# State-space layer's weights and tables loaded while the first attention layer runs, and the product of its output weights formed in that layer's drain

## The chip, the cores and the metric

The kernel runs on one NeuronCore of a Trainium2 chip, as one launch. The metric is the device time of that launch in microseconds (us), as the median of three runs. A core has five engines that run side by side and meet only at semaphores: PE (TensorE, matmuls and transposes), DVE (VectorE), ACT (ScalarE), POOL (GpSimd) and SP (SyncE, which here only issues DMA transfers; its issues stand as SPq in the trace). All transfers of this part go through the one queue that SP feeds, and share 16 DMA engines.

## The reference, cut to what matters

The program is four layers over `x` of 32 batches of 512 rows of 256 values. Each takes its input normalised and adds its result to `x`; only the first two touch the change.

```python
# layer 0, attention: one 512x512 table of edge types (adj) for each batch
x = x + _L0_gnn_ref(_layernorm(x, axis=-1), adj, L0_gnn_W, ...)
# layer 0, state space (mamba2)
x = x + _L0_ffn_ref(_layernorm(x, axis=-1), L0_ffn_W_in, L0_ffn_conv_w, L0_ffn_conv_b, L0_ffn_dt_bias,
                    L0_ffn_A_log, L0_ffn_D, L0_ffn_norm_w, L0_ffn_W_out, L0_ffn_W_lin, L0_ffn_b_lin)
...
# the end of the state-space layer: two products with constant matrices, one behind the other
Y = Y * jax.lax.rsqrt(jnp.mean(Y * Y, axis=-1, keepdims=True) + EPS) * norm_w
out = Y @ W_out
return out @ W_lin + b_lin
```

Because `norm_w`, `W_out` and `W_lin` are constant, the kernel forms `Wc = diag(norm_w) W_out W_lin` (512 x 256) once and multiplies by it alone.

## The kernel before

`build` calls five phases in turn: `first_attention_phase` (tiles `g0_...`, shown as `g_...` in the trace), `typed_attention_phase` (`ty_...`, whose body runs only on unusual edge types, and not for these inputs), `state_space_phase` (`ssm_...`), a second attention phase (also `g_...`) and an LSTM phase. Each phase is a block of its own: all engines meet at its end, then POOL clears its semaphores one by one (`Memory.clear`), and only then does the next block begin. Tiles of a phase are given up at its end, so a later phase can't be filled while an earlier one runs, unless its tiles are allocated outside both. Only `kept` lives across the first two.

In every phase each engine runs its own list, `period(b)`, in which operations of several batches are written out in a fixed order by hand; `b.wait(...)` puts a semaphore wait ahead of an operation. No planner sets anything; the order in the code is the order on the engine.

**First attention phase, the parts around the change.** SP, per period k: the edge table of batch k+4 (`load_adj`, L334, 1 MB, into the single buffer `ADJ`, so it waits until DVE and ACT have read the table before it), x of batch k+5 (`load_x`, L329), the result of batch k (`store`, L338). DVE reads `ADJ` in `make_mask` (L647, four 128x512 pieces). At the end, the last batch drains: PE ends with `outputs_turned` (L444), DVE with `squares_sum` (L711), POOL goes on with the layer norm (L806 to L820) and the last store follows. SP then waits for the stores to land, and the block ends.

**State-space phase, its setup.** SP issues x of batch 0 (L1216), then 35 small and large loads through `put` (L1214): all weights, biases and tables, two of them the same 8 values into eight row groups (`dtb`, `rate`), and then x of batch 1 (L1245). Every load of `put` counts on one semaphore, `w`. PE waits for all 35 before its first instruction, transposes `W_out` (L1266), waits for DVE's copies (L1606), and forms `W_out W_lin` (L1271). DVE casts the tables `head_rows` and `below` to bf16 (L1610 to L1614), repeats `Wdt` (L1617), scales the product into `Wc` (L1622), and only behind all this in its own list does it come to the first batch: `norm_stats` (L1632). From there the first batch goes DVE (statistics), POOL (L1816), ACT (normalised x, L1458), PE (L1280). `norm_stats` has its own semaphore for x, `x_loaded`; what keeps it from starting is its place in DVE's list:

```python
v.wait_ge(s["setup_a"], 1)
v.wait_ge(s["setup_v"], 5)
```

## Time and profile before

| | us |
|---|---|
| runs | 4551.28, 4548.48, 4547.19; median 4548.48 |
| profiled execution, its own time | 4549.33 |
| its span | 4547.5 |
| first attention phase, to the issue of its last store | 0 to 1018.3 |
| state-space phase, from its first instruction | 1033.95 |
| second attention phase, from its first instruction | 2417.53 |

The span is what the profiler saw of the engines, and the difference to the execution's own time (1.8 us) lies around it. Over the whole span PE is busy 88%, DVE 76%, ACT 63% and POOL 26% of the time. These shares say nothing on the stretch that the change touches, which is under 1% of the span; there one reads what each engine waited for.

### The profile page before, as it was taken

The numbers are of one execution on the slowest core, as the hardware profiler recorded it, in microseconds if no ns is written. First come the engines' busy times: TensorE is split into PE (matmuls) and PEld (weight loads), VectorE is DVE, ScalarE is ACT, GpSimd is POOL, SyncE is SP. The second block draws the span as 40 slices with busy tenths as digits, with TensorE's granted clock in tenths as the row PEclk, the third lists the DMA queues.
The fourth block names the chain that finished last, engine by engine and source line by source line (L and its number), as shares of the span: only waits on it lengthen the run. The fifth ranks groups of instructions, "written<-read, shape, count | busy, mean of one in ns | idle before, by whom it ended". The sixth has DMA issues, their size and how long they took to land. (4 is left out here: it accounts for less than half of the span.)

```text
span 4547.5 us, 142915 instructions
## 1 busy us (share of the span) xinstructions
PE 3986.8 (88%) x55570; PEld 2859.9 (63%) x55713; DVE 3476.3 (76%) x9096; ACT 2879.7 (63%) x7042; POOL 1181.9 (26%) x1028
## 2 busy tenths in 40 slices
PE   7999999975999999999997999938888888888882
PEld 5666666642666666666666777727777776777772
DVE  6999999975889888988886888825666666666666
ACT  6999999965888888888884777613333332333330
POOL 4777777760222222222221111000000000000000
PEclk9999999987999999999998999969999999999996
DMA  2222222211000000000003333321121111111115
GB/s 65 70 75 65 67 75 75 75 42 52 29 20 29 29 29 20 29 29 29 23 17 97 133 136 136 106 47 40 34 43 34 43 36 42 36 41 37 40 37 162
DMA packets 326430, 252.61 MB, mean 56 GB/s; under 512 B 171388, under 2 KB 289916, under 8 KB 323708
## 3 DMA queue, kind: packets, MB, share of 16 engines
q1 hardware_dynamic: 324220, 235.03, 17.7%
q8 instruction: 448, 7.34, 0.7%
q10 hardware_dynamic: 1536, 8.39, 0.5%
q14 instruction: 226, 1.85, 0.1%
HBM read 159.43 MB, written 67.11 MB: 50 GB/s over the span
## 5 line engine op out<-in xcount | busy, mean ns | idle before, releaser
L2510 PE MATMUL lstm_G_psum<-lstm_Whh,lstm_HT 128*32 128x192 f32 x8192 | 440.0, 332 | 266.8 <-DVE lstm_HT L2687 266.5
L2580 ACT ACTIVATE lstm_TC<-lstm_G_psum 128x192 f32<-128x192 f32 x512 | 170.5, 333 | 706.7 <-PE lstm_G_psum L2510 706.7
L1534 ACT ACTIVATE ssm_EX<-ssm_Z_psum,ssm_tok 128x256 f32<-128x256 f32 (+1 forms) x1024 | 371.8, 423 | 156.1 <-PE ssm_Z_psum L1364 86.3
L2510 PEld LDWEIGHTS lstm_G_psum<-lstm_Whh,lstm_HT 128*32 128x32 f32 x8192 | 214.2, 109 | 353.8 <-DVE lstm_HT L2687 320.2
L2502 PE MATMUL lstm_G_psum<-lstm_Wih,lstm_XT 128*32 128x192 f32 x8192 | 427.9, 327 | 0.0
L2676 DVE SCALAR_TENSOR_TENSOR lstm_AB<-lstm_TC 128x128 f32<-128x128 f32 x512 | 150.2, 293 | 335.1 <-ACT lstm_TC L2580 331.0
L2840 POOL TENSOR_SCALAR lstm_rstd<-lstm_mv 128x4 f32<-128x4 f32 x32 | 7.2, 225 | 1435.2 <-DVE lstm_mv L2670 1435.2
L541 ACT ACTIVATE g_PR<-g_S,g_nmax 128x512 f32<-128x512 f32 x512 | 367.9, 722 | 1.5 <-DVE g_nmax L676 1.5
L683 DVE COPY g_PT<-g_PT_psum 128x512 f32<-128x512 f32 x512 | 344.3, 683 | 26.1 <-PE g_PT_psum L424 21.4
L532 ACT ACTIVATE g_relu<-g_Z_psum,g_src 128x512 f32<-128x512 f32 x512 | 346.0, 682 | 20.5 <-PE g_Z_psum L417 20.4
L676 DVE CUSTOM_DVE_ANT_0 g_S<-g_Z_psum,g_relu 128x512 f32<-128x512 f32 x512 | 345.5, 684 | 10.2 <-ACT g_relu L532 8.6
L424 PEld LDWEIGHTS g_PT_psum<-g_ident,g_PR 128*128 128x128 f32 x2048 | 242.5, 141 | 135.9 <-ACT g_PR L541 53.8
L424 PE MATMUL g_PT_psum<-g_ident,g_PR 128*128 128x128 f32 x2048 | 303.1, 276 | 3.4 <-DVE g_PT L683 3.2
L1290 PE MATMUL ssm_J_psum<-ssm_XT,ssm_W_in 128*128 128x512 f32 x640 | 305.4, 600 | 0.5 <-DVE ssm_CV L1693 0.5
L2588 ACT ACTIVATE lstm_tc<-lstm_TC 128x64 f32<-128x64 f32 x512 | 131.3, 257 | 262.3 <-DVE lstm_TC L2679 262.3
L2502 PEld LDWEIGHTS lstm_G_psum<-lstm_Wih,lstm_XT 128*32 128x32 f32 x8192 | 285.3, 140 | 5.3
L1828 POOL TENSOR_TENSOR ssm_SS<-ssm_SS,ssm_SQ 128x512 f32<-128x512 f32 x96 | 123.8, 1290 | 611.6 <-ACT ssm_SQ L1547 606.6
L2683 DVE SCALAR_TENSOR_TENSOR lstm_H<-lstm_TO,lstm_tc 128x64 f32<-128x64 f32 x512 | 116.4, 227 | 201.6 <-ACT lstm_tc L2588 201.6
L435 PE MATMUL g_O_psum<-g_PT,g_HB 128*64 128x512 f32 x1024 | 262.7, 613 | 0.8 <-DVE g_PT L683 0.8
L1290 PE MATMUL ssm_A_psum<-ssm_XT,ssm_W_in 128*128 128x512 f32 x512 | 244.1, 599 | 1.4 <-DVE ssm_CV L1693 1.4
L1722 DVE SCALAR_TENSOR_TENSOR ssm_M<-ssm_EX,ssm_G 128x768 f32<-128x768 f32 x256 | 242.5, 948 | 0.1
L2058 PE MATMUL g_A_psum<-g_HS,g_PT 128*128 128x256 f32 x1024 | 241.8, 379 | 0.0
(303 smaller groups left out, 10832.6 us busy)
## 6 DMA issues: line engine op xcount, KB each, us to landing
g_ADJ<-in_adj SPq DMA_DIRECT2D x64, 1024.0 KB, 6.5
x<-g_XO SPq DMA_DIRECT2D x64, 512.0 KB, 5.4
g_X<-in_x SPq DMA_DIRECT2D x32, 512.0 KB, 4.3
ssm_X<-x SPq DMA_DIRECT2D x32, 512.0 KB, 3.9
x<-ssm_OUT SPq DMA_DIRECT2D x32, 512.0 KB, 2.9
g_X<-x SPq DMA_DIRECT2D x32, 512.0 KB, 4.4
lstm_raw<-x SPq DMA_DIRECT2D x1024, 16.0 KB, 1.8
lstm_U<-x SPq DMA_DIRECT2D x128, 128.0 KB, 3.5
```

Source lines behind the costliest of these rows:

```text
L424: ins = pe.transpose(PTb[n % 2][:, k * P:(k + 1) * P], PR[n % 4][:, k * P:(k + 1) * P], ident[:, :])
L435: ins = pe.matmul(Ob[hh * E:(hh + 1) * E, :], HB[b.slot][:, k, h * E:(h + 1) * E], PT[h][:, k, :], start=(k == 0), stop=(k == IT - 1), ski ...
L532: act.activation(relu[n % 4][:, :], score_bank(b, n)[:, :], ACT.Relu, scale=(1.0 - ALPHA) / ALPHA, bias=src[b.slot][:, t, HH * p + hh:HH * ...
L541: act.activation(PR[n % 4][:, :], S[n % 4][:, :], ACT.Exp, scale=-1.0, bias=nmax[:, n % 4:n % 4 + 1], accum_out=rsum[b.slot][:, t, HH * p ...
L676: v.tensor_tensor_reduce(S[n % 4][:, :], score_bank(b, n)[:, :], relu[n % 4][:, :], -1.0, 3e38, ALU.add, ALU.min, nmax[:, n % 4:n % 4 + 1] ...
L683: v.tensor_copy(PT[HH * p + hh][:, :, t * P:(t + 1) * P], PTb[n % 2][:, :].rearrange("p (k i) -> p k i", k=IT)).then_inc(s["ev"], 1)
L1290: ins = pe.matmul(BANK[f"p{k}"][:, :], W_in[:, kc, c:c + P], XT[:, kc, :], start=(kc == 0), stop=(kc == KC - 1))
L1534: ins = act.activation(EX[h % NE][:, col:col + n], Zb[c][:, i * CHUNK:i * CHUNK + n], ACT.Exp, bias=tok[b.slot][:, i, c, h:h + 1])
L1722: v.scalar_tensor_tensor(out=M[h % NM][:, :], in0=EX[h % NE][:, :], scalar=1.0, in1=G[b.slot][:, :], op0=ALU.min, op1=ALU.mult).then_inc(s ...
L2058: ins = pe.matmul(BANK[held][:, (t % 2) * D:(t % 2 + 1) * D], PT[t][:, k * P:(k + 1) * P], HS[b.slot][:, k, :], start=(k == 0), stop=(k == ...
L2502: pe.matmul(bank[32 * j:32 * (j + 1), 0:n], XT[c.slot][:, kc, :, t], Wih[:, kc, j, first:last], start=False, stop=False, skip_group_check= ...
L2510: ins = pe.matmul(bank[32 * j:32 * (j + 1), 0:last - first], HT[t % 2][:, 32 * kc:32 * (kc + 1)], Whh[:, kc, j, first:last], start=False, ...
```

## The change

Twelve tiles of the state-space phase (`ident`, `W_in`, `Wdt_rep`, `Wc`, `cw`, `cb`, `skip`, `dtb`, `rate`, `blin`, `keep`, `allowed`) move into a dictionary `ready` that is allocated beside `kept` and lives from the first phase to the end of the state-space phase. SP fills them in the first attention phase: `next_weights` adds 31 loads behind the stores of periods 2 to 12. `W_out` is loaded over `WT`, a tile of the first phase's own setup, and `W_lin` and `norm_w` into new tiles there. Behind its last period PE transposes `W_out` and forms the product, DVE copies and scales it into `Wc`. The tables `head_rows` and `below` are now handed over as bf16 in pairs, so that they are loaded straight into `head_bf` and `rows` by three loads in the state-space phase (655 KB in place of 1.3 MB, no casts); PE waits for these three only in `spread`, its first use. `Wdt` repeated is loaded four times in place of one load and two copies. The state-space phase's DVE begins `norm_stats` behind four memsets and a wait on ACT's exponent of `rate`.

```diff
+        W_lin = m.sb("W_lin", [P, KC, D])
+        WoT = m.sb("WoT", [P, KC, 2 * D])
+        normw = m.sb("normw", [P, 4])
...
+        WT = m.sb("WT", [P, H, D])
+        W_out = WT
...
+            def next_weights(part):
+
+                w_in = nw["W_in"].rearrange("(c k) e -> k c e", k=P)
+                if part == 0:
+                    sp.wait_ge(s["setup_pe"], 2)
+                    put(W_out[:, :, :], nw["W_out"].rearrange("(c k) e -> k c e", k=P))
+                    put(W_lin[:, :, :], nw["W_lin"].rearrange("(c k) e -> k c e", k=P))
+                    put(normw[:, :], nw["norm_w"].rearrange("(c k) -> k c", k=P), allow_slow_non_contiguous=True)
+                if part == 1:
+                    put(nk["W_in"][:, :, :], w_in[:, :, 0:nk["W_in"].shape[2]])
+                if part == 2:
+                    put(nk["allowed"][:, :], consts["allowed"])
+                    put(nk["keep"][:, :], consts["part_masks"])
+                    put(nk["cw"][:, :, :], nw["conv_w"].rearrange("(c k) e -> k c e", k=P))
+                if part == 3:
+                    put(nk["cb"][:, :], nw["conv_b"].rearrange("(c k) -> k c", k=P), allow_slow_non_contiguous=True)
+                    put(nk["blin"][:, :], nw["b_lin"].rearrange("(o d) -> o d", o=1).to_broadcast([P, D]))
+                if part == 4:
+                    for h in range(2):
+                        put(nk["skip"][64 * h:64 * (h + 1), :],
+                            nw["D"].rearrange("(o c h) -> o c h", o=1, h=2)[:, :, h].to_broadcast([64, 4]),
+                            allow_slow_non_contiguous=True)
+                if part in (5, 6):
+                    for r in (0, 1):
+                        k = 2 * (part - 5) + r
+                        put(nk["Wdt_rep"][:, :, 8 * k:8 * (k + 1)], w_in[:, :, nk["W_in"].shape[2]:])
+                if part in (7, 8, 9, 10):
+                    for k in (2 * (part - 7), 2 * (part - 7) + 1):
+                        put(nk["dtb"][8 * k:8 * (k + 1), :], nw["dt_bias"].rearrange("(h o) -> h o", o=1))
+                        put(nk["rate"][8 * k:8 * (k + 1), :], nw["A_log"].rearrange("(h o) -> h o", o=1))
+
             for k in range(-5, nb + 0):
                 period(Batch(None, k, SLOTS))
+                if 2 <= k < 13:
+                    next_weights(k - 2)
+            assert n == N_W
+            sp.wait_ge(s["nw"], 16 * N_W)
...
+            pe.wait_ge(s["nw"], 16 * N_W)
+            pe.wait_ge(s["s"], ITEMS * nb)
+            for kc in range(KC):
+                for c in range(4):
+                    ins = pe.transpose(Zb[kc][:, c * P:(c + 1) * P], W_out[:, c, kc * P:(kc + 1) * P], ident[:, :])
+            ins.then_inc(s["wo_pe"], 1)
+            pe.wait_ge(s["wo"], 2)
+            pe.wait_ge(s["ev"], ITEMS * nb)
+            for c in range(4):
+                for kc in range(KC):
+                    ins = pe.matmul(PTb[c // 2][:, (c % 2) * D:(c % 2 + 1) * D], WoT[:, kc, c * P:(c + 1) * P],
+                                    W_lin[:, kc, :], start=(kc == 0), stop=(kc == KC - 1))
+            ins.then_inc(s["wc_pe"], 1)
...
+            v.wait_ge(s["wo_pe"], 1)
+            for kc in range(KC):
+                v.tensor_copy(WoT[:, kc, :], Zb[kc][:, :]).then_inc(s["wo"], 1)
+            v.wait_ge(s["wc_pe"], 1)
+            for c in range(4):
+                v.tensor_scalar(nk["Wc"][:, c, :], PTb[c // 2][:, (c % 2) * D:(c % 2 + 1) * D], normw[:, c:c + 1], None,
+                                ALU.mult).then_inc(s["wc"], 1)
...
             sp.dma_start(X[0][:, :, :], xv[0]).then_inc(x_loaded[0], 16)
-            put(ident[:, :], consts["identity"])
+            sp.dma_start(head_bf[:, :].bitcast(F32), consts["head_rows"]).then_inc(s["w"], 16)
             for k in range(2):
-                put(allowed[:, 2 * k * P:(2 * k + 1) * P], consts["upto"])
...
+                sp.dma_start(rows[k][ROWS:P, :, :].rearrange("p k l -> p (k l)").bitcast(F32), consts["below"][ROWS:P, :]
+                             ).then_inc(s["w"], 16)
...
             def spread(b, h, c):
+                if b.off == 0 and h == 0:
+                    pe.wait_ge(s["w"], 48)
```

**DVE, from the end of the first attention phase's list into the typed phase, before** (names as in the code, buffer numbers left out):

```order
L711 TENSOR_REDUCE g_ssq<-g_SQ 128x16
L224 UNCONDITIONAL_BRANCH
L968 UNCONDITIONAL_BRANCH
L971 MEMSET ty_ones 128x128
L972 MEMSET ty_half 128x16
```

and now:

```order
L780 TENSOR_REDUCE g_ssq<-g_SQ 128x16
L835 COPY g_WoT<-g_Z_psum 128x512 x2
L838 TENSOR_SCALAR kept_Wc<-g_PT_psum,g_normw 128x256 x4
L232 UNCONDITIONAL_BRANCH
L1045 UNCONDITIONAL_BRANCH
L1048 MEMSET ty_ones 128x128
```

The two copies and the four products with `norm_w` stand behind the last operation of the drain, `squares_sum`.

**DVE, from the start of the state-space phase to its first batch, before:**

```order
L1600 MEMSET ssm_ST 128x512 x2
L1601 MEMSET ssm_ones 128x256
L1602 MEMSET ssm_allowed 128x128
L1603 MEMSET ssm_half 128x16
L1606 COPY ssm_Y<-ssm_Z_psum 128x512 x2
L1610 CAST ssm_head_bf<-ssm_M 128x768 x3
L1610 CAST ssm_head_bf<-ssm_M 128x256
L1612 CAST ssm_rows<-ssm_EX 64x128
...
L1617 COPY ssm_Wdt_rep<-ssm_Wdt 128x32 x2
L1622 TENSOR_SCALAR ssm_Wc<-ssm_J_psum,ssm_normw 128x256 x4
L1632 BN_STATS ssm_stats<-ssm_X 128x6 x4
```

and now:

```order
L1625 MEMSET ssm_ST 128x512 x2
L1626 MEMSET ssm_ones 128x256
L1627 MEMSET ssm_half 128x16
L1634 BN_STATS ssm_stats<-ssm_X 128x6 x4
L1638 BN_AGGR ssm_mv<-ssm_stats 128x2 x4
```

Everything between the memsets and the statistics of batch 0 has left the list.

**SP, around the second period that carries extra loads.** Before, the store of one batch is followed at once by the edge table:

```order
L334 DMA g_ADJ<-in_adj 128x4x512
L329 DMA g_X<-in_x 128x4x256
L338 DMA x<-g_XO 128x4x256
L334 DMA g_ADJ<-in_adj 128x4x512
```

and now, periods 2 and 3:

```order
L358 DMA x<-g_XO 128x4x256
L329 DMA g_WT<-in_L_ffn_W_out 128x4x256
L329 DMA g_W_lin<-in_L_ffn_W_lin 128x2x256
L329 DMA g_normw<-in_L_ffn_norm_w 128x4x1
L354 DMA g_ADJ<-in_adj 128x4x512
L349 DMA g_X<-in_x 128x4x256
L358 DMA x<-g_XO 128x4x256
L329 DMA kept_W_in<-in_L_ffn_W_in 128x2x1152
L354 DMA g_ADJ<-in_adj 128x4x512
```

Between a store and the edge table stand now one to four loads, in eleven periods running.

## Rows read from the trace of the kernel before

**Rows 1.** The page: busy tenths of PE in 40 slices of the span.

```profile
PE   7999999975999999999997999938888888888882
```

**Rows 2.** Waits from 1018 to 1110 us: engine, line, releaser: total, times, longest.

```profile
ACT ssm_rate L1452 <- DMA ssm_rate<-in_L_ffn_A_log: 52.0, 1, 52.0
```

**Rows 3.** Timeline, start of the state-space phase: start, duration, engine and operation.

```profile
1034.09 0.39 SPq L1216 DMA_DIRECT2D ssm_X<-x  x1
...
1035.34 0.07 DVE L1603 MEMSET ssm_half<- 128x16 f32 x1
...
1041.41 3.16 SPq L1214 DMA_DIRECT2D ssm_cb<-in_L_ffn_conv_b  x1
1044.62 2.23 SPq L1214 DMA_DIRECT2D ssm_normw<-in_L_ffn_norm_w  x1
1046.89 1.36 SPq L1214 DMA_DIRECT2D ssm_blin<-in_L_ffn_b_lin  x1
...
1055.49 0.29 SPq L1214 DMA_DIRECT2D ssm_rate<-in_L_ffn_A_log  x1
```

**Rows 4.** Timeline, setup work of the state-space phase and its first batch.

```profile
1058.97 1.97 PE L1266 MATMUL ssm_Z_psum<-ssm_ident,ssm_OUT 128*128 128x128 f32 x8 [32.27 <-DMA ssm_rate<-in_L_ffn_A_log]
1060.97 1.29 DVE L1606 COPY ssm_Y<-ssm_Z_psum 128x512 f32<-128x512 f32 x2 [25.56 <-PE ssm_Z_psum L1266]
...
1062.32 5.16 PE L1271 MATMUL ssm_J_psum<-ssm_Y 128*128 128x256 f32 x16 [1.38 <-DVE ssm_Y L1606]
...
1067.52 1.66 DVE L1622 TENSOR_SCALAR ssm_Wc<-ssm_J_psum,ssm_normw 128x256 f32<-128x256 f32 x4 [2.67 <-PE ssm_J_psum L1271]
1069.27 1.41 DVE L1632 BATCH_NORM_STATS2 ssm_stats<-ssm_X 128x6 f32<-128x256 f32 x4
...
1075.47 1.09 PE L1280 MATMUL ssm_J_psum<-ssm_ident,ssm_XN 128*128 128x128 f32 x4 [7.99 <-ACT ssm_XN L1458]
...
1080.55 1.39 DVE L1632 BATCH_NORM_STATS2 ssm_stats<-ssm_X 128x6 f32<-128x256 f32 x4
...
1102.17 0.33 PE L1359 MATMUL ssm_Z_psum<-ssm_rows,ssm_head_bf 128*128 128x384 bf16 x1
```

**Rows 5.** Tile view of ssm_X, whole span: time from issue to landing.

```profile
DMA to landing us min/median/max: 3.6/3.9/4.0
```

**Rows 6.** Tile view of g_ADJ, 100 to 1000 us, the same.

```profile
DMA to landing us min/median/max: 5.2/5.8/6.6
```

**Rows 7.** Timeline, SP's issues around period 3 of the first phase.

```profile
241.76 0.50 SPq L338 DMA_DIRECT2D x<-g_XO  x1
245.05 0.37 SPq L334 DMA_DIRECT2D g_ADJ<-in_adj  x1
```

**Rows 8.** Timeline, DVE's first read of that edge table.

```profile
254.13 0.52 DVE L647 TENSOR_SCALAR g_MASK<-g_ADJ 128x512 bf16<-128x512 int32 x1
```

**Rows 9.** Stretches: length, busy us of each engine, PEclk, DMA share, GB/s.

```profile
155.00:160.00 5.00, 4.95 (x28) 2.49 (x26) 4.32 (x16) 4.15 (x10) 4.84 (x4) 1.00 1.01 341
...
1045.00:1050.00 5.00, 0.00 (x0) 0.00 (x0) 0.00 (x0) 0.00 (x0) 0.00 (x0) 0.50 0.79 201
```

**Rows 10.** Timeline, drain of the first attention phase.

```profile
998.87 1.42 PE L444 MATMUL g_A_psum<-g_ident,g_OT 128*128 128x128 f32 x8
...
1006.98 1.22 DVE L711 TENSOR_REDUCE g_ssq<-g_SQ 128x16 f32<-128x1024 f32 x1 [3.45 <-ACT g_SQ L560]
...
1015.98 2.34 POOL L820 TENSOR_TENSOR g_XO<-g_G,g_XB 128x1024 f32<-128x1024 f32 x1
1025.49 0.17 DVE L971 MEMSET ty_ones<- 128x128 f32 x1 [17.29 <-PEq L118]
```

**Rows 11.** DMA view, 1018 to 1024 us: KB, us from issue to landing.

```profile
x<-g_XO SPq DMA_DIRECT2D x1, 512.0 KB, 2.9
```

**Rows 12.** Stretches, the state-space phase's first matmuls: columns as in rows 9.

```profile
1072.00:1082.00 10.00, 5.75 (x19) 3.14 (x20) 1.81 (x6) 4.10 (x8) 1.05 (x3) 0.50 0.00 0
1082.00:1090.00 8.00, 7.53 (x18) 3.11 (x17) 6.04 (x14) 6.72 (x9) 4.02 (x5) 0.98 0.22 66
```

More of the change, by code:

```diff
@@ L310, in _, with put @@
         def _(sp):
+            n = 0
+            def put(tile, src, **kw):
+                nonlocal n
+                n += 1
+                sp.dma_start(tile, src, **kw).then_inc(s["nw"], 16)
             sp.dma_start(X[0][:, :, :], xv[0]).then_inc(x_loaded[0], 16)
@@ L1159, in state_space_phase @@
         RES = [m.sb(f"RES{k}", [P, T, D]) for k in range(2)]
-        W_out, WoT = OUT, Y[0][:, 0:KC, :]
-        below = EX[0][:, 0:P]
-        W_lin = Y[0][:, KC, :].rearrange("p (c d) -> p c d", c=KC)
         Zb = [m.ps(f"Z{k}") for k in range(2)]
@@ L1167, in state_space_phase @@
         A0, A1 = (m.ps(f"A{k}") for k in range(2))
-        names = ("w setup_pe setup_v setup_a st mv rs shift xn xt_pe xt dt_pe raw sp_a sp_b sp_c dt run fall left dtw high "
+        names = ("w setup_v setup_a st mv rs shift xn xt_pe xt dt_pe raw sp_a sp_b sp_c dt run fall left dtw high "
                  "rest mid rows tt_pe tok pj conv tap silu zs g_pe g bt_pe bt xd_pe xd xs st_pe ste z ex m cs y y1 y2 "
@@ L1262, in _ @@
         def _(pe):
-            pe.wait_ge(s["w"], 16 * N_W)
-            for kc in range(KC):
-                for c in range(CT):
-                    ins = pe.transpose(Zb[kc][:, c * P:(c + 1) * P], W_out[:, c, kc * P:(kc + 1) * P], ident[:, :])
-            ins.then_inc(s["setup_pe"], 1)
-            pe.wait_ge(s["setup_v"], 2)
-            for c in range(CT):
-                for kc in range(KC):
-                    ins = pe.matmul((J0, J1)[c // 2][:, (c % 2) * D:(c % 2 + 1) * D], WoT[:, kc, c * P:(c + 1) * P],
-                                    W_lin[:, kc, :], start=(kc == 0), stop=(kc == KC - 1))
-            ins.then_inc(s["setup_pe"], 1)
-            pe.wait_ge(s["setup_v"], 5)
+            pe.wait_ge(s["setup_v"], 1)
             def xn_turned(b, kc):
@@ L1601, in _ @@
             v.memset(ones[:, :], 1.0)
[L1602 to L1624 removed]
+            v.memset(half[:, :], -0.5).then_inc(s["setup_v"], 1)
             v.wait_ge(s["setup_a"], 1)
[L1626 removed]
             def norm_stats(b):
```

103 lines of the change are left out of this document (25 added, 78 removed).

## The prediction

> **What bounds the kernel now.** The page's slices come first [rows 1]: PE is busy nine tenths in most slices of 113.7 us; the dip to 7 and 5 in the ninth and tenth (909 to 1137 us) is where the first attention phase hands over to the state-space phase. The shares of the whole span can't price it, so I went to the waits of that stretch. ACT waited 52.0 us, and what ended it was the last load of the setup, `rate` [rows 2]. The timeline says why it was so late: SP issued the first load at 1034.09 and the last of the 35 at 1055.49 [rows 3]. It is SP's issue time that is long, above all that of `cb` (3.16 us for 2.5 KB) and `normw` (2.23 us), not the transfer of the bytes. The last load landed, PE started at 1058.97, and then came a chain in which PE and DVE take turns: transposes 1.97 us, copies 1.29, product 5.16, scaling 1.66. Only behind it does DVE reach the statistics of batch 0 at 1069.27 [rows 4]. All later work hangs on that instruction: phases are separated by a meeting of all engines, and within the phase the first batch passes DVE, POOL, ACT, PE in turn. So each us by which 1069.27 moves forward against the phase's start is a us of the kernel, and each us by which the first phase ends later is one lost.
>
> **What the state-space phase gains.** In the new list DVE has four memsets, the last at 1035.34 + 0.07 [rows 3], and a wait for ACT's exponent, which now finds its input loaded. What remains is x of batch 0. It is issued first, at 1034.09, before and after. A load of that tile lands 3.6 to 4.0 us after its issue, median 3.9 [rows 5]; the statistics start at 1034.09 + 3.9 = 1038.0, in place of 1069.27: **31.3 us** earlier.
>
> The Trainium skill, "DMA: Bandwidth & Descriptors", section on the anatomy of one DMA, gives 2.0 us plus bytes over 436 GB/s, measured on the other, software-driven path. For 512 KB that is 3.2 us, and the sum would be 32.0 us; the row of this very tile goes before it.
>
> Behind x of batch 0 now stand 655 KB of tables and two small pieces, then x of batch 1. If the DMA engines mixed these with x of batch 0, it would land late by up to 0.66 MB + 0.52 MB at 341 GB/s [rows 9] = 3.5 us. That is the upper bound; before, too, other loads followed at once behind the first. I take nothing, since these rows of the tile show a spread of only 0.4 us. The other deadlines are far: x of batch 1 is wanted 11.3 us behind the statistics of batch 0 (1080.55 - 1069.27), and the tables by PE's first `spread`, 32.9 us behind (1102.17 - 1069.27) [rows 4], when all of 1.7 MB takes 5 us at 341 GB/s.
>
> PE's clock gives nothing back. Its granted clock was 0.50 (1.2 GHz) in 1072 to 1082 us, and 0.98 in 1082 to 1090 [rows 12]: the setup's product had not left it warm for the first batch. Without it the first batch starts on the same 1.2 GHz, so I carry that stretch over as it is.
>
> **What the first phase pays, 1: its loop.** DVE fills its list almost without a gap there, so a late edge table costs its lateness. The pattern repeats every 29.8 us; period 3 stands for all. The store is issued at 241.76 for 0.50 us, the table at 245.05: SP has 2.8 us free between them [rows 7]. The table lands 5.2 to 6.6 us after issue, median 5.8 [rows 6], at 250.85, and DVE first reads it at 254.13 [rows 8]: 3.3 us of slack. The new loads:
> - `W_in`, 1.18 MB, one issue (period 3). At 341 GB/s, the rate of a stretch in which the DMA engines were full [rows 9], it takes 3.5 us. If all of it comes before the table, the table lands at 254.3: 0.2 us late.
> - `W_out`, `W_lin`, `normw`, 0.79 MB (period 2): 2.3 us of transfer. Their issues take about 0.5 + 0.5 + 2.23 us, 0.5 more than the gap, and that runs beside the transfer. Lands inside the slack.
> - `cb` and `blin` (period 5): 3.16 + 1.36 us of issue [rows 3], 1.7 over the gap, and 0.13 MB more, 0.4 us. Inside.
> - the other eight periods: at most four issues of 0.3 us each (as the last `rate` load shows [rows 3]) or two of 0.7, inside the 2.8 us, and next to no bytes.
>
> So 0.2 us. The lower bound is nothing. The upper one takes the poorest rate of a stretch at work, 201 GB/s [rows 9], where the small pieces of the setup were moved: `W_in` 5.9 us, 2.6 too late; `W_out` and the rest 3.9 + 0.5 us, 1.1 too late; `cb` period 1.7 + 0.7, inside. Together 3.7 us.
>
> **What the first phase pays, 2: its drain.** The eight transposes start when PE is through, at 998.87 + 1.42 = 1000.3 [rows 10], and are done by 1002.3 even at the price of rows 4. DVE's copies stand behind L711, which ends at 1006.98 + 1.22 = 1008.2. From there 1.29 + 5.16 + 1.66 us of rows 4 (at 1.2 GHz; PE has idled 6 us) give 1016.3, with 0.3 us for three hand-overs 1016.6. Beside it POOL works until 1015.98 + 2.34 = 1018.3 [rows 10] on the last batch; its store lands 2.9 us later [rows 11], at 1021.2. The block can't end before. So the product costs nothing; its cover is 4.6 us, and what it is longer than that would be paid in full. DVE and POOL ran side by side in the whole loop, so I add nothing for POOL.
>
> **3: the semaphores.** From 1021.2 to the typed phase's first instruction at 1025.49 [rows 10] are 4.3 us, in which 53 semaphores are cleared and the engines meet: at most 0.08 us each. Five more are 0.4 us; one fewer in the state-space phase gives 0.1 back. Net 0.3. (Bounds 0 and 0.4.)
>
> **The sum.** 31.3 - 0.2 - 0 - 0.3 = 30.8 us. Against the profiled execution's own 4549.33 us that gives 4518.5; this execution lies 0.9 over the median of the runs, 4548.48, and for that median I predict **4517.7 us**.
>
> **The rivals.**
> - *Late edge tables.* The loads come at the head of each table's transfer, and DVE waits. For: the DMA engines are full in the 5 us of rows 9, and `W_in` has just the slack. Against: three periods only have something to move. With the upper bounds, 3.7 in place of 0.2, the time is 4521.2. The Trainium skill, "DMA: Bandwidth & Descriptors", section on queues, rings and completion order, says that an engine takes descriptors in ring order, which would put the whole of `W_in` ahead of the table; the sum above already does so.
> - *Code or queue at the start.* Before, ACT, PE and POOL had 25 us and more of waiting at the phase's start, under which anything slow of a start is hidden, their first instructions included; only DVE and SP show that they run at once. If PE, ACT or POOL were late, or x of batch 0 mixed with the tables, 1 to 4 us of the 31.3 go: 4519 to 4522, say 4520.2 with the middle of it. Against: PE's first work is wanted only 10 us after the start (1075.47 - 1069.27 + 3.9 [rows 4]), and ACT's, the exponent, 3.9 us after it.
> - *The drain is too short a cover.* If a step of the product takes 4.6 us more than in rows 4, the remainder is paid. Nothing in the profile speaks for it; 4518 to 4521.
> - *The change doesn't do what it says*: something else, invisible under the wait, holds the first batch back by over 22 us, and the time is within 0.2% of before. In the list of waits nothing but the loads ended a wait longer than those of the chain itself.
> - *The other sign.* One mechanism could do it: the edge table late in all eleven periods. It decides from 30.8 / 11 = 2.8 us of waiting in each, which is 6.1 us of lateness beyond today's landing, slack included; to end 0.2% slower, 3.6 and 6.9. The eight light periods would have to be as bad as that with 1.4 us of issue in a gap of 2.8, for a time of 4557 (11 x 3.6 = 40 us, less the 30.8). Against it: all the small loads of the setup had landed 3.5 us after the last was issued (1055.49 [rows 3] to PE's start at 1058.97 [rows 4]).
>
> **How the numbers follow.** Forecast 0.76, late tables 0.08, slow start 0.08, drain 0.03, no effect 0.03, other sign 0.02. What a measurement of this kernel can tell from no change is about 0.2%, 9.1 us (the three runs lie 4.1 us apart). The first four cases are all faster by more: 0.95; same 0.03; slower 0.02. The range takes in the bounds: downwards the fastest landing (0.3), no lateness and no price of semaphores (0.5) and half the spread of runs (2), so 4514.9; upwards the bounds of the tables (3.5) and of the mixing (3.5), which need not fall together, and the runs' spread. I give **4514 to 4524**.
>
> **What would show it.** In the changed kernel's profile: the last store of the first phase issued within 0.5 us of 1018.3, if the loop lost nothing; no waits of DVE for the edge table, and the table's landing longer in periods 2 and 3; the product's scaling ending at about 1016.6, before the store lands; the state-space phase's first statistics some 3.9 us behind SP's first issue there, at about 1038.3 (the first phase 0.2 later, the semaphores); the distance from these statistics to the second attention phase's start the same as now, 2417.53 - 1069.27 = 1348.3 us. The prediction is wrong if that distance grows, if the first phase's end moves, or if the first load lands late.

## The result, and the profile after

| | before | changed |
|---|---|---|
| median of the runs, us | 4549.54 (4 runs, 4547.19 to 4551.28) | 4518.00 (4 runs, 4513.31 to 4523.99) |
| profiled execution: own time, span | 4549.33, 4547.5 | 4515.77, 4513.9 |
| the same again, beside the experiments | 4548.80 (11 runs) | 4519.81 (5 runs, 4515.89 to 4523.94) |

The ratio is 0.9935 with a 95% interval of 0.9923 to 0.9948, and 0.9937 (0.9923 to 0.9950) the second time. The changed kernel is 0.65% faster, 31.5 us by the medians of the first comparison and 29.0 by those of the second, at 4518.0 where 4517.7 was predicted. In the page's slices of 112.8 us the dip of PE in the ninth and tenth is less deep, 8 and 6 for 7 and 5 [rows 1]; the other digits that differ, 8 4 for 9 3 in the 26th and 27th, are the last phase's start, which moved against the slices:

```profile
PE   7999999986999999999997999848888888888882
```

The timeline of the changed kernel at the state-space phase's start (start, duration, engine, line and operation, idle before it and its releaser) answers to [rows 3, 4]:

```profile
1026.65 0.17 DVE L1048 MEMSET ty_ones<- 128x128 f32 x1 [9.02 <-PEq L118]
...
1035.27 0.38 SPq L1271 DMA_DIRECT2D ssm_X<-x  x1
...
1035.69 0.50 SPq L1272 DMA_DIRECT2D ssm_head_bf<-in_head_rows  x1
1036.24 1.15 SPq L1274 DMA_DIRECT2D ssm_rows<-in_below  x2
...
1036.70 0.07 DVE L1627 MEMSET ssm_half<- 128x16 f32 x1
1037.43 0.59 SPq L1280 DMA_DIRECT2D ssm_X<-x  x1
1039.10 1.41 DVE L1634 BATCH_NORM_STATS2 ssm_stats<-ssm_X 128x6 f32<-128x256 f32 x4 [2.32 <-DMA ssm_X<-x]
```

The wait that ended in the last of 35 loads is gone. What DVE waits for now is x of batch 0, for 2.32 us, and the statistics start 3.83 us behind SP's first issue, where before it was 1069.27 - 1034.09 = 35.18 us [rows 3, 4]. That is 31.35 us.

The drain of the first phase, beside [rows 10]:

```profile
1000.88 1.04 PE L562 MATMUL g_Z_psum<-kept_ident,g_WT 128*128 128x128 f32 x8
...
1007.74 1.22 DVE L780 TENSOR_REDUCE g_ssq<-g_SQ 128x16 f32<-128x1024 f32 x1 [3.45 <-ACT g_SQ L629]
1008.88 1.28 DVE L835 COPY g_WoT<-g_Z_psum 128x512 f32<-128x512 f32 x2
...
1010.21 5.72 PE L568 MATMUL g_PT_psum<-g_W_lin,g_WoT 128*128 128x256 f32 x16 [8.29 <-DVE g_WoT L835]
...
1015.97 1.66 DVE L838 TENSOR_SCALAR kept_Wc<-g_PT_psum,g_normw 128x256 f32<-128x256 f32 x4 [5.81 <-PE g_PT_psum L568]
1016.75 2.34 POOL L897 TENSOR_TENSOR g_XO<-g_G,g_XB 128x1024 f32<-128x1024 f32 x1
```

The product's scaling ends at 1017.63, POOL's last sum at 1019.09, and the store that follows takes 2.9 us: the product is inside. But POOL's sum starts at 1016.75, 0.77 us later than before [rows 10]. The loop lost that much, and the timeline shows where. It is in the sixth period, in which `skip` is loaded (2 x 64 partitions x 4 elements of 4 bytes):

```profile
331.75 2.10 SPq L329 DMA_DIRECT2D kept_skip<-in_L_ffn_D  x2
334.50 0.37 SPq L354 DMA_DIRECT2D g_ADJ<-in_adj  x1
...
340.17 4.84 POOL L856 TENSOR_SCALAR g_XN<-g_X,g_mv,g_rstd 128x256 f32<-128x256 f32 x4
344.13 0.49 DVE L716 TENSOR_SCALAR g_MASK<-g_ADJ 128x512 bf16<-128x512 int32 x1 [0.48 <-DMA g_ADJ<-in_adj]
344.97 2.35 POOL L897 TENSOR_TENSOR g_XO<-g_G,g_XB 128x1024 f32<-128x1024 f32 x1
345.14 2.47 DVE L716 TENSOR_SCALAR g_MASK<-g_ADJ 128x512 bf16<-128x512 int32 x1
```

The table landed 9.6 us behind its issue (5.5 in the same period before). DVE waited 0.48 us for it; its second mask then came 0.17 us behind the start of POOL's sum and took 2.47 us instead of 0.41, until POOL was done. The period is 31.98 us long (334.50 to 366.48), the others 29.80. So 2.2 us were lost here. In the profile of before and in nine of the other twelve, DVE waits 1.24 us for PE shortly before the loop's end (at 990.84 in before); in this execution it doesn't, and the rest of the loop is 1.4 us shorter for it. The net is 0.77.

All pieces of the two profiled executions: first phase +0.77; from POOL's sum to the typed phase +0.39; typed phase +0.02; start to statistics -31.35; statistics to the second attention phase -0.36 (1347.90, before 1348.26); that phase -0.36; the last phase, which the change doesn't touch, -2.7. Together -33.6, the difference of the spans. The last phase alone took 1584.3 to 1591.1 us in the fourteen executions profiled for this study, so single executions compare to 3 us at best, and what is said below of single us is read from pieces, not from ends.

### The profile page after: what moved, and what is told of

Its sections match the earlier page's. It is cut to its first block and busy times, and to the rows that moved or that the text cites. A ratio compares the mean times of both kernels' runs of the same rounds, so it can differ in the third digit from the quotient of the medians.

```text
span 4513.9 us, 143053 instructions
## 1 busy us (share of the span) xinstructions
PE 3992.5 (88%) x55713; PEld 2860.4 (63%) x55713; DVE 3475.4 (77%) x9083; ACT 2879.2 (64%) x7042; POOL 1182.1 (26%) x1028
## 5 line engine op out<-in xcount | busy, mean ns | idle before, releaser
L745 DVE CUSTOM_DVE_ANT_0 g_S<-g_Z_psum,g_relu 128x512 f32<-128x512 f32 x512 | 345.4, 684 | 10.3 <-ACT g_relu L601 8.8
L479 PEld LDWEIGHTS g_PT_psum<-kept_ident,g_PR 128*128 128x128 f32 x2048 | 241.9, 141 | 136.2 <-ACT g_PR L610 53.8
L1314 PE MATMUL ssm_J_psum<-ssm_XT,kept_W_in 128*128 128x512 f32 x640 | 305.3, 599 | 0.5 <-DVE ssm_CV L1695 0.5
L479 PE MATMUL g_PT_psum<-kept_ident,g_PR 128*128 128x128 f32 x2048 | 302.6, 275 | 3.5 <-DVE g_PT L752 3.3
L1314 PE MATMUL ssm_A_psum<-ssm_XT,kept_W_in 128*128 128x512 f32 x512 | 244.1, 599 | 1.4 <-DVE ssm_CV L1695 1.4
```

Of the source, the lines that this page charges most:

```text
L479: ins = pe.transpose(PTb[n % 2][:, k * P:(k + 1) * P], PR[n % 4][:, k * P:(k + 1) * P], ident[:, :])
L745: v.tensor_tensor_reduce(S[n % 4][:, :], score_bank(b, n)[:, :], relu[n % 4][:, :], -1.0, 3e38, ALU.add, ALU.min, nmax[:, n % 4:n % 4 + 1] ...
L1314: ins = pe.matmul(BANK[f"p{k}"][:, :], W_in[:, kc, c:c + P], XT[:, kc, :], start=(kc == 0), stop=(kc == KC - 1))
```

## The experiments

Four questions: which part of the wait was paid for what (A), whether the drain and the semaphores cost what they seem to (B), what the sixth period is (C), and whether the answers add up to a better kernel (D). The changed kernel stood beside them once more. The intervals of the ratios of some versions overlap with the changed kernel's; there it is the pieces of the trace that tell them apart, and differences of medians only go along.

> The changed kernel once more, beside the experiments. Theory: the 4.5 us spread of its first four runs, 2.6 of which between fastest and slowest lie in the last phase's serial recurrence, is noise between executions; the ratio comes out at 0.993 to 0.994 and the profile again shows the first norm statistics of the state-space phase 3.8 to 3.9 us behind SP's first issue. If the two small skip loads are what delays the sixth edge table (landing 9.6 us after its issue, 5.5 before), the same table is late again, by 3.5 us or more; if that was an accident of one execution it lands in 5.2 to 6.6 us.

Measured: median 4519.81, ratio 0.9937. Statistics 4.21 us behind SP's first issue, above the 3.8 to 3.9 expected. The sixth table landed 8.5 us behind its issue, between the two cases set out (3.0 us later than before, not 3.5); DVE didn't wait for it, and the period was 29.78 us.

### A. Loads or product

**W_out and W_lin back in the state-space phase** (product too; edit shortened).

```diff
+            sp.dma_start(W_out[:, :, :], nw["W_out"]...).then_inc(s["wo"], 16)   # behind x of batch 0
+            sp.dma_start(W_lin[:, :, :], nw["W_lin"]...).then_inc(s["wo"], 16)
+            sp.dma_start(normw[:, :], nw["norm_w"]..., ...).then_inc(s["wo"], 16)
...
+            pe.wait_ge(s["wo"], 16 * 3)        # PE: transposes and product at the phase's start
```

> W_out, W_lin, norm_w and their product go back to the state-space phase, all other loads stay early. Theory (statistics wait for the last of loads and product in a chain): the three loads are issued by 2.9 us after x (0.38 + 0.50 + 1.54 + 0.56 from the issue rows), land at about 1041.5, and the chain of 10.1 us (1.97 + 1.29 + 5.16 + 1.66) follows, so the statistics start 16.5 to 18 us behind SP's first issue instead of 3.8: 13 to 14 us slower than the changed kernel, 4531 to 4532, ratio 0.9960. Rival (the number of loads and the bytes, some 20 us of issue, were the whole cost and the product ran beside something): within 5 us of the changed kernel, 4518 to 4523.

Measured: 4535.62 (6 runs), ratio 0.9968 (0.9956 to 0.9980), 15.8 us slower than the changed kernel.

```profile
1038.37 0.39 SPq L1244 DMA_DIRECT2D ssm_X<-x  x1
...
1045.87 1.97 PE L1278 MATMUL ssm_Z_psum<-kept_ident,ssm_OUT 128*128 128x128 f32 x8 [14.57 <-DMA ssm_normw<-in_L_ffn_norm_w]
1047.87 1.29 DVE L1618 COPY ssm_Y<-ssm_Z_psum 128x512 f32<-128x512 f32 x2 [8.00 <-PE ssm_Z_psum L1278]
1049.21 6.66 PE L1283 MATMUL ssm_J_psum<-ssm_Y 128*128 128x256 f32 x16 [1.38 <-DVE ssm_Y L1618]
1055.91 1.66 DVE L1621 TENSOR_SCALAR kept_Wc<-ssm_J_psum,ssm_normw 128x256 f32<-128x256 f32 x4 [6.75 <-PE ssm_J_psum L1283]
1057.49 1.39 DVE L1630 BATCH_NORM_STATS2 ssm_stats<-ssm_X 128x6 f32<-128x256 f32 x4
```

The chain theory holds: three loads keep PE from starting for 7.5 us, the chain follows, and the statistics come 19.1 us behind SP's issue. The statistics are 1.1 us above their expected range and the median is 3.6 us above its own: PE started 1.3 us later than expected, the chain was 1.5 us longer because the product took 6.66 us, and the way from the statistics to the second attention phase grew to 1350.59. The rival, within 5 us of the changed kernel, is out.

**Only the product in the state-space phase**, all loads early. PE's and DVE's parts of the product move from the drain to the phase's start (shortened; W_out, W_lin and norm_w stay in tiles of their own):

```diff
-            pe.wait_ge(s["nw"], 16 * N_W)        # first phase, drain
-            ...                                  # transposes, product
+            for kc in range(KC):                 # state-space phase, first on PE
+                for c in range(CT):
+                    ins = pe.transpose(Zb[kc][...], W_out[...], ident[:, :])
```

> All loads stay early, only the product of W_out and W_lin is formed at the start of the state-space phase. Theory: no load is waited for, the chain of 10.1 us starts at once and ends later than x's landing at 3.8 us, so the statistics start 10.3 to 10.8 us behind the phase's first instruction, 6.5 to 7 us later than in the changed kernel: 4524.5 to 4525, ratio 0.9945. Rival (the matrix engine works earlier, so its clock rises earlier and some of it is given back in the first batch): 2 to 5 us slower than the changed kernel.

Measured: 4528.46 (4 runs), ratio 0.9954 (0.9939 to 0.9969), 8.7 us slower than the changed kernel. Transposes start with the phase (1038.55), the product takes 6.63 us, and the statistics are 11.6 us behind SP's first issue, 7.8 us later than in the changed kernel. The 7.8 us are 0.8 to 1.3 more than expected, again by the longer product. The rival is out: nothing of PE's clock came back in the first batch. Two windows of this kernel, 12 to 16 us behind its statistics (columns as in [rows 9]):

```profile
1062.12:1064.12 2.00, 2.00 (x3) 0.79 (x3) 1.04 (x7) 0.24 (x1) 0.76 (x2) 0.50 0.00 0
1064.12:1066.12 2.00, 2.00 (x5) 0.88 (x4) 0.60 (x1) 1.40 (x2) 1.83 (x4) 0.81 0.01 4
```

And of the changed kernel, as far behind its own:

```profile
1051.10:1053.10 2.00, 2.00 (x5) 0.77 (x5) 1.04 (x7) 0.49 (x2) 0.76 (x2) 0.81 0.00 0
1053.10:1055.10 2.00, 2.00 (x6) 0.93 (x5) 1.40 (x2) 1.97 (x3) 1.83 (x4) 1.00 0.02 4
```

In both versions with the product at the phase's start the clock rises to its upper level (1.00, 2.4 GHz) 2 us later counted from the statistics, and the way to the second attention phase is 2.7 us longer (1350.65 and 1350.59, against 1347.90). The later rise is only a part of that: at the statistics of the fourth batch the two are 0.85 us behind. The rest, 1.7 us, is lost at the phase's end, in the last batch's product with `Wc`, during which the clock fell. In this kernel, the window (clock 0.60) and PE's row:

```profile
2382.00:2384.00 2.00, 1.66 (x4) 1.39 (x5) 0.29 (x1) 0.95 (x2) 1.43 (x2) 0.60 0.00 0
```

```profile
2382.34 5.41 PE L1410 MATMUL ssm_A_psum<-kept_Wc,ssm_Y 128*128 128x256 f32 x16 [2.05 <-DVE ssm_Y L1739]
```

and in the changed one, with the clock at 1.00:

```profile
2370.46 3.72 PE L1423 MATMUL ssm_A_psum<-kept_Wc,ssm_Y 128*128 128x256 f32 x16 [2.06 <-DVE ssm_Y L1744]
```

That the early product is what moves the rise and the fall is not shown. In the kernel of D, which has no product there, the clock was also still at 0.50 from 12 to 14 us behind the statistics, and the fourth batch's were 0.77 us behind; in the kernel before, with the product there, the way was 1348.26.

So, of 31.35 us, counted from the typed phase's start to the statistics: the product is 7.8 (20.27 - 12.45), its three loads another 7.1 (27.40 - 20.27), and the rest, 16.4 us, was the other loads. These prices hold for taking things away in this order: the product alone costs 7.8 and not its 11.6 because x of batch 0 is on its way for 3.8 us beside it.

### B. Cover and semaphores

**The product four times over in the drain.**

```diff
+            for again in range(4):
                 for c in range(4):
                     for kc in range(KC):
```

> The product in the drain is formed four times over (same result). Theory: the chain of the drain ended at 1017.63, the last store landed at about 1022, so there are 4.4 us of cover; three more products at 5.7 us each at the lower clock (2.9 each if the clock rises meanwhile) add 8.6 to 17.2 us, of which 4.2 to 12.8 us show in the time. Rival (the block's end does not wait for the chain alone, or the cover is larger than the store shows): under 3 us.

Measured: 4524.80, ratio 0.9948 (0.9932 to 0.9963). Matmuls 16.05 us instead of 5.72, 10.33 more. From POOL's last sum to the typed phase 15.59 us instead of 9.90, 5.69 more. So 4.6 us of the addition were hidden, as much as the cover of the prediction:

```profile
1011.56 16.05 PE L569 MATMUL g_PT_psum<-g_W_lin,g_WoT 128*128 128x256 f32 x64 [8.29 <-DVE g_WoT L836]
...
1018.10 2.35 POOL L898 TENSOR_TENSOR g_XO<-g_G,g_XB 128x1024 f32<-128x1024 f32 x1
1027.66 1.66 DVE L839 TENSOR_SCALAR kept_Wc<-g_PT_psum,g_normw 128x256 f32<-128x256 f32 x4 [16.15 <-PE g_PT_psum L569]
1033.69 0.17 DVE L1049 MEMSET ty_ones<- 128x128 f32 x1 [4.38 <-PEq L118]
```

**Forty more semaphores in the first phase.**

```diff
+        unused = [m.sem(f"unused{k}") for k in range(40)]
```

> Forty semaphores that nothing uses are added to the first phase, cleared with the others at its end. Theory (each clear takes POOL 0.08 us, as five more took 0.39 us in the two traces): from the last POOL operation of the phase to the next phase's memset 10.7 to 10.9 us instead of 7.56, 3.2 us slower than the changed kernel. Rival (clears are hidden behind the end of the block on the other engines, and the 0.39 us was chance): less than 0.5 us.

Measured: 4526.86, ratio 0.9947 (0.9932 to 0.9962). From POOL's last sum (1020.08) to the typed phase's first instruction 12.78 us, 2.88 more than 9.90:

```profile
1032.86 0.17 DVE L1049 MEMSET ty_ones<- 128x128 f32 x1 [12.09 <-PEq L118]
```

A clear costs 0.072 us, and nothing hides it. The median moved by more, 7.1 us against the second one of the changed kernel. In the profiled execution the sixth period was 4.5 us too long (table under C), which would account for the rest; the other three runs have no trace.

**The clears shared by five engines**, in all phases.

```diff
+            share = lambda k: self.sems[k::5]
...
+            @block.vector
+            def _(v):
+                for sem in share(1):
+                    v.sem_clear(sem)             # and so on ACT, PE and SP; POOL keeps share(0)
```

> At every phase's end the semaphores are cleared by all five engines, a fifth each, instead of by POOL alone. Theory (a clear takes 0.08 us of POOL and the next phase starts behind the last one): the first phase has about 60, so some 48 fewer in a row, 3.8 us less there and 7.56 becomes 3.7; over the five phases 10 to 18 us faster than the changed kernel. Rival (other engines clear more slowly or the barrier around the clears is what takes the time): within 2 us.

Measured: 4512.17, ratio 0.9923 (0.9909 to 0.9936), 7.6 us faster than the changed kernel's second median. From POOL's sum to the typed phase 7.60 us instead of 9.90, so 2.3 us and not the 3.8 expected: clears by the others are not free, or the meeting takes its share; which, I did not separate. By pieces: 2.3, then 1.2 to the statistics, 2.6 in the state-space phase, 2.0 in the second attention phase; 8.1, short of the expected 10. The median fits that, but its interval overlaps with the changed kernel's, so the gain rests on the pieces.

### C. The sixth period

The issue of each edge table is 29.80 us behind the one before, unless something stops DVE. The table of the sixth period, in profiled executions; those of the changed kernel and of the five of A and B have `skip` ahead of it:

| execution | sixth table lands, us behind issue | to the next issue, us |
|---|---|---|
| before | 5.5 | 29.81 |
| changed | 9.6 | 31.98 |
| changed, again | 8.5 | 29.78 |
| W_out in state space, product in state space | 10.7, 11.4 | 34.34, 34.32 |
| shared clears, 40 semaphores, product x4 | 10.4, 10.9, 10.5 | 34.29, 34.33, 34.30 |
| skip late | 6.0 | 29.80 |
| bulk late | 9.9 | 33.58 |

The price comes in steps, nothing, 2.2 or 4.5 us, for a landing 8.5, 9.6 and 10.4 us or more behind the issue. "Bulk late" fits in: SP's long issues had put its table's own issue 0.7 us behind the 29.80, so it landed 10.6 us behind the regular moment, and the two periods together took 4.5 us too long. At the higher step it is the first mask that runs into POOL's sum, at the lower one, in the changed kernel, the second. The changed kernel's four runs spread 10.7 us and the first four of before 4.1, but thirteen later ones of before spread 9.4; whether the sixth period has a part in the spread is not shown.

**skip late.** The pair goes to the last periods, behind which no table is loaded.

```diff
-                if part == 4:
+                if part == 27:                   # and: if 2 <= k < 13 or k == 29
```

> The two skip loads (64 partitions by 4 elements of 4 bytes each) move from the sixth period to the last ones, behind which no edge table is loaded. Theory (they hold up the transfer behind them): the edge table of that period lands in 5.2 to 6.6 us again instead of 9.6, DVE waits for no table, no mask operation takes 2.47 us, and the loop's last POOL operation is at 1016.5 to 1018.5 instead of 1019.09: 0.5 to 2.3 us faster than the changed kernel. Rival (accident of that execution): a late table or a long mask operation appears at another place or nowhere, and the time is within 0.5 us of the changed kernel.

Measured: 4516.18 (5 runs, 4515.45 to 4520.60), ratio 0.9932 (0.9918 to 0.9945). In time that can't be told from the changed kernel (0.9937); in the trace it can: landing 6.0 us, no wait of DVE for a table, POOL's last sum at 1014.36. That is 2.4 us before the changed kernel's and 2.1 earlier than expected: 2.2 of it are the sixth period and 1.5 an earlier third table (last section), less the 1.4 of DVE's wait near the loop's end, which is there again. The DMA traffic tells why the table was late. In the windows of the changed kernel it was issued at 334.50, and then the DMA engines stood nearly still for 2 us (last two columns: their busy share, and GB/s), with most of the table still to come:

```profile
332.00:334.00 2.00, 2.00 (x10) 1.07 (x10) 1.93 (x9) 2.00 (x6) 2.00 (x1) 1.00 0.59 154
334.00:336.00 2.00, 2.00 (x16) 0.82 (x12) 1.42 (x5) 1.41 (x4) 1.92 (x2) 1.00 1.04 355
336.00:338.00 2.00, 2.00 (x13) 0.97 (x10) 1.97 (x7) 1.74 (x5) 1.92 (x2) 1.00 0.05 2
338.00:340.00 2.00, 2.00 (x12) 1.56 (x11) 1.82 (x8) 2.00 (x5) 1.92 (x3) 1.00 0.31 107
```

In this kernel, with the table issued at 332.84, there is no such hole:

```profile
332.40:334.40 2.00, 2.00 (x16) 0.82 (x12) 1.43 (x4) 1.41 (x4) 1.92 (x2) 1.00 1.00 353
334.40:336.40 2.00, 1.95 (x12) 0.97 (x10) 1.97 (x8) 1.74 (x5) 1.92 (x2) 1.00 0.97 296
336.40:338.40 2.00, 2.00 (x12) 1.61 (x12) 1.82 (x8) 2.00 (x5) 1.92 (x3) 1.00 0.58 224
```

**skip in all eleven periods.**

```diff
-                if part == 4:
+                if part >= 0:
```

> The two skip loads are issued in each of the eleven periods ahead of the edge table instead of in one. Theory (the small broadcast holds up the table behind it): tables land in 8.5 to 10 us in all eleven, DVE waits 0.5 us or more for each and the loop is 5 to 25 us longer. Rival (they delay only together with something else, or the wait is taken up by slack): landings under 7 us or waits of nothing, loop within 1 us of the changed kernel's.

Measured: 4557.39 (9 runs), ratio 1.0023 (1.0013 to 1.0032). Landings 7.8 to 13.9 us. From the issue of period 1's table (155.68 here, two tables ahead of the first that stands behind a pair) to POOL's last sum the loop took 897.90 us, against 860.32 in the kernel with skip late: 37.6 more, 3.4 for each period. (DVE's wait near the loop's end is missing here too; without the 1.4 us that this gives back it would be 39.0.) I had expected at most 25, and landings of 10 us at most. DVE waited 20.3 us for tables, and seven masks took 1.5 to 2.7 us, each until about 0.3 us behind the end of POOL's sum of two inputs. One of them:

```profile
360.38 4.84 POOL L856 TENSOR_SCALAR g_XN<-g_X,g_mv,g_rstd 128x256 f32<-128x256 f32 x4
364.41 0.43 DVE L716 TENSOR_SCALAR g_MASK<-g_ADJ 128x512 bf16<-128x512 int32 x1 [0.54 <-DMA g_ADJ<-in_adj]
365.19 2.36 POOL L897 TENSOR_TENSOR g_XO<-g_G,g_XB 128x1024 f32<-128x1024 f32 x1
365.35 2.48 DVE L716 TENSOR_SCALAR g_MASK<-g_ADJ 128x512 bf16<-128x512 int32 x1
```

**The same loads with sources of their own.**

```diff
+                for h in range(2 if part < 27 else 0):
+                    put(like_skip[64 * h:64 * (h + 1), :],
+                        nw["norm_w"].rearrange("(c k) -> k c", k=P)[64 * h:64 * (h + 1), :],
```

> As the kernel with the skip loads in all eleven periods, with one thing changed: the 2 x 64 x 4 elements of 4 bytes in each period come from norm_w, each from an address of its own, in place of D, where 64 partitions read the same four addresses (the real skip loads stand in the last periods; the extra loads fill a tile that nothing uses). Theory A (many readers of the same few addresses are slow): tables land in 5.5 to 8 us, the loop's last POOL operation is at 1014 to 1018 and the time within 3 us of the kernel with the skip loads late, 4516 to 4519. Theory B (512 elements of 4 bytes are slow whatever their source): tables land at 9.5 to 11 us in all eleven and the loop ends near 1053, 4557.

Measured: 4517.83, ratio 0.9932 (0.9915 to 0.9949). SP's issues take as long as those of `skip` (2.10 us for the two), but tables land in 5.1 to 8.0 us, the longest behind W_in, DVE waits for none, and the loop takes 860.34 us. The packets themselves show the difference. The first line is the DMA view of 2 us in the changed kernel's sixth period (336 to 338 us), the second that of 1 us here, in the same period (333 to 334):

```profile
DMA packets 205, 0.00 MB, mean 2 GB/s; under 512 B 202, under 2 KB 205, under 8 KB 205
DMA packets 796, 0.31 MB, mean 309 GB/s; under 512 B 525, under 2 KB 767, under 8 KB 796
```

Here the small packets are through in about 1 us, beside 309 GB/s of other traffic; there they come at 101 per us, and next to nothing moves beside them. Theory A holds: it is not the small elements, of which there are as many, but what they read, 64 partitions the same few addresses. (The two sources are also different tensors, of 32 bytes and 2 KB; one of 32 bytes without repeated reads was not tried.)

**Bulk late.** W_out, W_lin, norm_w and W_in together in the sixth period, skip in the last ones.

```diff
-                if part == 0:                    # W_out, W_lin, norm_w
+                if part == 4:
...
-                if part == 1:                    # W_in
+                if part == 4:
```

> No small broadcast loads ahead of a table (skip stands in the last periods), but W_out, W_lin, norm_w and W_in, 1.97 MB, all in the sixth period instead of in the second and third. Theory (a table that lands more than about 9 us behind its issue costs a wait, and the mask operation that is late then stands behind POOL's x + beta sum for 2.2 us, whatever made the table late): landing 9.5 to 11 us, one mask operation of 2 to 2.7 us, the period 32 to 34.4 us long instead of 29.80: 2 to 5 us slower than the kernel with the skip loads late, 4518 to 4521. Rival (only the small broadcast loads do that): period of 29.8 us.

Measured: 4521.77, ratio 0.9942 (0.9925 to 0.9958). Landing 9.9 us, a wait of 1.48, a mask of 2.47 beside POOL's sum, the period 33.58 us long:

```profile
343.20 2.35 POOL L897 TENSOR_TENSOR g_XO<-g_G,g_XB 128x1024 f32<-128x1024 f32 x1
343.36 2.47 DVE L716 TENSOR_SCALAR g_MASK<-g_ADJ 128x512 bf16<-128x512 int32 x1 [1.48 <-DMA g_ADJ<-in_adj]
```

The median is 0.8 us above the expected range. What makes the table late doesn't matter; that it is late does.

**POOL's sum behind the mask**, on top of skip in all eleven periods.

```diff
+                if t == 1:
+                    ins.then_inc(s["half_mask"], 1)      # DVE, make_mask
...
+                        (b + 3).wait(g, s["half_mask"], 1, 1)   # POOL, layernorm stage 3
```

> As the kernel with the skip loads in all eleven periods, and POOL's last sum of a batch waits until DVE has made the second mask of the new table, so that the two never run together. Theory (a period's loss of 3.6 us is the wait for the table, 1.8 us, and as much again from the mask operation that is held up by POOL's sum of two inputs until that ends): no mask operation over 0.6 us; the loop loses the waits alone, 15 to 22 us instead of 39, 4535 to 4540. Rival (the long mask operation only shows the late table, or POOL's delay costs as much): 4554 or more.

Measured: 4538.79 (10 runs), ratio 0.9978 (0.9968 to 0.9988), 18.6 us faster than without the wait. The tables are as late as before (8.2 to 13.6 us), DVE waits 23.6 us for them, but no mask takes over 0.6 us, and the loop takes 885.08 us: 24.8 lost instead of 37.6.

```profile
361.78 0.43 DVE L716 TENSOR_SCALAR g_MASK<-g_ADJ 128x512 bf16<-128x512 int32 x1 [2.28 <-DMA g_ADJ<-in_adj]
362.73 0.42 DVE L716 TENSOR_SCALAR g_MASK<-g_ADJ 128x512 bf16<-128x512 int32 x1
363.38 2.37 POOL L901 TENSOR_TENSOR g_XO<-g_G,g_XB 128x1024 f32<-128x1024 f32 x1 [2.52 <-DVE g_MASK L716]
```

Of the 12.8 us between the two loops (14.2 with the 1.4 from above), 11.9 are the time by which the seven long masks exceed 0.42 us each. Another 2.2 of the 18.6 lie ahead of that stretch, where the kernels don't differ. The rival is out; the loop loses 24.8 where 15 to 22 were expected, since the waits for tables, 23.6 us, remain.

### D. A better version

Skip in the last periods, clears shared, and x of the state-space phase's first batch loaded in the first phase, behind that batch's store.

```diff
+                if k == 29:
+                    sp.wait_ge(stored[0], 16)
+                    put(nk["X0"][:, :, :], ov[0])
...
-            sp.dma_start(X[0][:, :, :], xv[0]).then_inc(x_loaded[0], 16)
+            sp.sem_inc(x_loaded[0], 16)
```

> Three things together on top of the changed kernel: the skip loads in the last periods, the semaphore clears of every phase shared by the five engines, and x of the state-space phase's first batch loaded in the first attention phase (again in the typed phase where that one runs). Theory: the clears give 8.6 us (sum of the phases in the trace of the kernel with shared clears alone), the skip loads 1.5 to 5.8 us in the sixth period, and the statistics start behind the phase's memsets instead of behind x's landing, 2 to 2.4 us earlier: 4504 to 4508, ratio 0.991. Rival (what is no longer waited for at one place is waited for at the next): 4512 or more, no better than the shared clears alone.

Measured: 4501.90 (4 runs, 4501.25 to 4505.34), ratio 0.9898 (0.9881 to 0.9914). 17.9 us under the changed kernel's second median, 10.3 under the shared clears alone, and 2.1 below the expected range. Its interval lies below that of the changed kernel.

```profile
1019.88 0.17 DVE L1075 MEMSET ty_ones<- 128x128 f32 x1 [7.19 <-PEq L118]
...
1027.31 0.35 SPq L1299 DMA_DIRECT2D ssm_head_bf<-in_head_rows  x1
1027.42 1.02 DVE L1652 MEMSET ssm_ST<- 128x512 f32 x2 [6.15 <-SPq L1298]
...
1028.66 0.41 DVE L1661 BATCH_NORM_STATS2 ssm_stats<-kept_X 128x6 f32<-128x256 f32 x1
```

The statistics stand right behind the memsets, 8.78 us behind the typed phase's first instruction instead of 12.45. The sixth period is 29.81 us.

## Why the prediction was right, step by step

- **Statistics 3.9 us behind the first issue; 31.3 us gained.** Measured 3.83 and 31.35. In the ten profiled executions in which x is loaded there and no product stands ahead it was 3.78 to 4.21, at most 0.3 us above the median landing of before [rows 5], so the tables behind it in the queue cost it no more than that; the 3.5 us of mixing were not there. The rival of a slow start falls too: the way from the statistics on was 1347.90 (1348.3 predicted).
- **PE's clock gives nothing back.** Right, and for the changed kernel it takes nothing either. In the two kernels with the product back, 2.7 us are lost behind the statistics to a later rise and an earlier fall of the clock, from a cause that stays open.
- **The loop, 0.2 us.** The sum's size was right in one execution (0) and too small in the others (2.2 and 4.5 us), and the reason was another. W_in, on which I had put the 0.2, made its table land 7.4 to 8.8 us behind the issue in the nine executions with nothing else there, and DVE never waited for it. The step that failed is "the other eight periods: at most four issues of 0.3 us each [...] or two of 0.7, inside the 2.8 us, and next to no bytes". It prices a load by issue time and bytes, and the skip loads are cheap by both; what they cost is the stop of the transfers behind them. Before, that stood under ACT's wait of 52.0 us [rows 2], so no row of before priced it, and the bound for these periods should have come from there.
- **"A late edge table costs its lateness."** It costs that and a collision. In the good case the second mask ends 0.2 us ahead of POOL's sum (mask 344.46 to 344.87, sum 345.09, in the second execution of the changed kernel). The slack behind the landing is 3.3 us, as read from [rows 7, 8], but behind that there is 0.2 us to a step of 2 us. The rival of late tables had the mechanism with 0.08 and a time of 4521.2; it came about in six of the seven profiled executions with `skip` in the sixth period. It deserved more. In the changed kernel's own execution the 2.2 us showed as 0.77, since the end of the loop gave 1.4 back.
- **The other sign.** It needed 3.6 us of waiting in each of eleven periods for 4557. The version with the skip pair in all eleven has about that, 3.4 us and 4557.4, part of it waiting and part the held mask: the mechanism is real, and what kept the change from it is that the pair stands in one period.
- **Drain free, cover 4.6 us.** Right: 4.6 us hidden of 10.3. The chain ended at 1017.63 and not 1016.6, 0.8 of it because the whole drain was later. The product's duration isn't a constant, though: 5.16 before, 5.72 in the drain, 6.63 and 6.66 at the phase's start, by when in it the clock rises. The 5.16, taken as a price at 1.2 GHz, were not that: the clock was 0.50 in the product's first 2.7 us (1062.30 to 1065.00 in before) and 1.00 from 1065.50 to its end.
- **Semaphores, 0.4 less 0.1.** 0.39 for five, 0.072 each by the forty. The 0.1 belongs to the end of the state-space phase, where the one semaphore fewer is cleared; the way from the statistics across that end was 0.36 us shorter, 0.16 of it by the fourth batch already, so the runs don't separate it.

The time was met because the term of 31 us was right to 0.1. That the median came within 0.3 us is luck: the second median is 4519.81, the small terms were off by up to 4 us, and the last phase alone varies by 6.8.

## What to carry to other kernels

Loads that are wanted at a phase's start belong into the phase before, where the queue and the transfers have room, and what they cost there is read from the deadline of the transfer behind them, not from their bytes. A broadcast of a few 4-byte elements to many partitions goes where nothing urgent follows it. And where a list is packed to 0.2 us, ask what the late instruction will run beside: two engines in each other's way can double the price of lateness, as here, where a wait of 20.3 us cost the loop 37.6.

## What the runs showed of the hardware

- Two loads of 64 partitions x 4 elements of 4 bytes from the same few addresses made a 1 MB load behind them land 8.5 to 11.4 us after its issue, instead of 5.5 to 6.0 (7.8 to 13.9 in the version with eleven such pairs); as many elements with addresses of their own did not (5.1 to 8.0).
- DVE's mask operation (one input in SBUF, int32 to bf16, 0.42 us alone) ended 0.28 us behind POOL's sum of two inputs (128x1024) and not sooner, in all fourteen cases in which the sum still had 1.2 us or more to run. Beside POOL's `g_XN` (one input, four operations in 4.83 to 5.27 us) it took 0.63 us at most, and inside POOL's `g_ssq` (two inputs of 128x16, 2.93 us) 0.42, thirty times in each trace. The Trainium skill, "SBUF — State Buffer", section "SBUF: two separate sides", says that DVE, in its 2-port modes or with two inputs in SBUF, and GpSimd share a pair of ports by a lock that the one that starts first holds for its whole instruction. The trace agrees for the sum; for the `g_XN` operations, 1.2 us each, and for `g_ssq` it shows no such wait, and in three executions the mask's start was level with the sum's or up to 0.06 us ahead of it, and it was held up all the same. In which mode the mask ran no trace shows.
- A semaphore clear on POOL takes 0.072 us, and the first phase's end, with 58 of them, pays for all; shared by five engines, it was 2.3 us shorter.
- The way to the third table's issue is 1.3 to 2.2 us longer in some executions than in others, of kernels that don't differ there (issued at 65.1 to 65.4 or at 63.3 to 63.9). Its cause stays open.
